# Moving the first tile's q and k into the last slots of a first attention, and the expert selection within them

## What is computed

```python
x = x + tanh(g_xattn[0]) * attention0(layernorm(x), ctx)    # 32 query, 8 key/value heads of 128, rope, softmax
x = x + tanh(g_ffn[0])  * ffn0(layernorm(x))                # 4-bit weights, 8-bit activations, silu(gate) * up, down
x = x + tanh(g_xattn[1]) * attention1(layernorm(x), ctx)    # over the 512 channels of each sequence
x = x + tanh(g_ffn[1])  * moe(layernorm(x))                 # base product + 4 of 16 low-rank experts with a router

def attention1(x, init):                     # per sequence, init is the context, 64 x 512
    q = Wq @ init + bq;  k = Wk @ init + bk  # 64 x 512 each
    A = softmax(q.T @ k)                     # 512 x 512
    v = Wv @ x + bv
    return A applied to v

def moe(x):
    y = x @ W_base.T + b_base
    contribs = (x @ A_e.T) @ B_e.T * 2       # rank 8, for the four active experts e
    alpha = softmax(log(prior[active] + 1e-12) + router(x)[active])
    return y + sum_e alpha_e * contribs_e
```

## Time and profile before

| | us |
|---|---|
| median of 3 timed runs | 848.2 (847.93 to 850.28) |
| the profiled execution | 856.15 |
| its span, first to last instruction | 854.3 |
| TensorE busy in the span | 816.7 (96%) |
| VectorE | 559.4 (65%) |
| ScalarE | 464.3 (54%) |
| GpSimd | 503.1 (59%) |
| mean granted TensorE clock | 0.983 of full |

### The profile page before, as it was taken

The page is one execution under the profiler, slowest core; times in us unless marked ns, Lnnn a source line. Parts: engine busy times, 40 slices in busy tenths (PEclk is TensorE's granted clock), DMA queues, the critical chain, the costliest instruction groups (busy, mean ns, idle before and its releaser), DMA issues. The chain is left out here.

```text
span 854.3 us, 13778 instructions
## 1 busy us (share of the span) xinstructions
PE 816.7 (96%) x5009; PEld 657.5 (77%) x5025; DVE 559.4 (65%) x1041; ACT 464.3 (54%) x874; POOL 503.1 (59%) x432
## 2 busy tenths in 40 slices
PE   6799999999999999999999999998968999999996
PEld 5688888888888888888888888886835677777785
DVE  3767656656566465564565545454779999999852
ACT  2465445554455454444544444332368899888761
POOL 1557744666555676456665557533057787877762
PEclk9999999999999999999999999998889999999998
DMA  8520331422413133131231104128044313321300
GB/s 260 136 87 26 111 87 38 125 54 76 124 35 100 44 89 102 38 94 43 65 109 43 38 5 26 50 37 305 2 111 119 83 48 90 85 76 25 87 26 25
DMA packets 74307, 66.77 MB, mean 78 GB/s; under 512 B 35920, under 2 KB 53552, under 8 KB 73856
## 3 DMA queue, kind: packets, MB, share of 16 engines
q1 hardware_dynamic: 73280, 65.55, 28.3%
q10 hardware_dynamic: 960, 0.33, 0.1%
HBM read 49.04 MB, written 6.34 MB: 65 GB/s over the span
## 5 line engine op out<-in xcount | busy, mean ns | idle before, releaser
L917 DVE SCALAR_TENSOR_TENSOR x_res<-bank,gate,x_res 128x512 f32<-128x512 f32 x128 | 95.7, 747 | 96.9 <-PE bank L505 96.5
L1155 POOL TENSOR_TENSOR prob<-prob,row_inv 128x512 f32<-128x512 f32 x32 | 33.5, 1046 | 197.5 <-DVE row_inv L913 197.5
L1141 POOL TENSOR_TENSOR rope_swap<-rope_swap,trig 128x512 f32<-128x512 f32 x80 | 103.6, 1295 | 35.5 <-ACT rope_swap L688 35.5
L78 PE MATMUL bank<-xnT_hi,wq_hi 128*128 128x512 f32 (+1 forms) x264 | 106.0, 402 | 1.0 <-DVE xnT_lo L852 1.0
L500 PE MATMUL bank<-wo_hi,oT_hi 128*128 128x512 f32 x256 | 102.9, 402 | 3.7 <-DVE x_res L917 3.5
L80 PE MATMUL bank<-xnT_hi,wq_lo 128*128 128x512 f32 (+1 forms) x264 | 103.7, 393 | 0.0
L79 PE MATMUL bank<-xnT_lo,wq_hi 128*128 128x512 f32 (+1 forms) x264 | 103.1, 391 | 0.0
L501 PE MATMUL bank<-wo_lo,oT_hi 128*128 128x512 f32 x256 | 102.4, 400 | 0.0
L888 DVE TENSOR_TENSOR rope_cos<-bank,trig 128x512 f32<-128x512 f32 x80 | 54.6, 683 | 71.5 <-PE bank L80 71.5
L687 ACT COPY rope_swap<-bank 64x512 f32<-64x512 f32 x80 | 46.8, 585 | 88.5 <-DVE rope_cos L888 87.9
L1147 POOL TENSOR_TENSOR q_rope<-rope_cos,rope_swap 128x512 f32<-128x512 f32 x64 | 83.4, 1303 | 5.0
(11 more groups left out here) (225 smaller groups left out, 1954.5 us busy)
## 6 DMA issues: line engine op xcount, KB each, us to landing
wq_raw<-in_L_xattn_wq SPq DMA_DIRECT2D x16, 512.0 KB, 4.2
wo_raw<-in_L_xattn_wo SPq DMA_DIRECT2D x16, 512.0 KB, 3.9
xn<-in_L_ffn_Wd SPq DMA_DIRECT2D x16, 256.0 KB, 3.4
b_ctx<-in_ctx SPq DMA_DIRECT2D x32, 128.0 KB, 2.7
b_k_twice<-b_qk_hi SPq DMA_DIRECT2D x32, 128.0 KB, 2.4
w_T_dram<-w_out SPq DMA_DIRECT2D x28, 128.0 KB, 2.3
w_T<-w_T_dram SPq DMA_DIRECT2D x2, 1376.0 KB, 8.1
xn<-in_L_ffn_Wg SPq DMA_DIRECT2D x10, 256.0 KB, 4.0
```

The lines of the kernel that those rows point to most:

```text
L78: pe.matmul(out, a_hi, b_hi, start=first, stop=False)
L917: dve.scalar_tensor_tensor(out=K.x[:, t, :], in0=wo_ps[t % 2][:, :], scalar=K.gate[:, 0:1], in1=K.x[:, t, :], op0=ALU.mult, op1=ALU.add).t ...
L1141: pool.tensor_tensor(out=sw, in0=sw, in1=sin_b, op=ALU.mult).then_inc(s_rope, 1)
```

## The change

Seven edits, and the lists of the tail written anew.

1. VectorE's expert selection, both halves, stands after the four accumulates of slot 30 and not among them.
2. ScalarE's split of tile 0's context (first_split_hi, twice) moves from the tail to the end of its slot 30, the low part from the tail's head on GpSimd to its queue behind the last normalise; GpSimd's reciprocal root for the first four x tiles now stands behind it, and the four clears of k_lo behind that.
3. q and k of tile 0 (first_qk) are made between the first and second tile sum of unit 31 in the attention's own banks; first_hi_qk and first_lo_qk follow on ScalarE and VectorE.
4. SyncE issues tile 0's ten copies in the first block.
5. low_T is cut in two: channels 0 and 1 after the second tile sum, 2 and 3 and the spread products after the third. first_x_transpose and low_b_select come between that and the fourth sum, no longer at the end.
6. ln_prior is ScalarE's last step of the first block; the second then starts with a table load for tanh.
7. qk_lo and ctx_raw/x3 change places in SBUF.

```diff
@@ sync, after load_context of tile 0
+            sp.wait_ge(M.s_k_zero, 4)
+            for par in range(2):
+                sp.wait_ge(M.s_qk_lo[par], 1)
+                duplicate_tile(sp, M, 0, par)
@@ tensor
-                    if tl == 1 and between is not None:
-                        between()
+                    if between is not None:
+                        between(tl)
...
+            def first_qk(par):
+                if par == 0:
+                    pe.wait_ge(s_w_qkv, 4)
+                    pe.wait_ge(s_w_qkv_lo, 1)
+                    pe.wait_ge(s_oT_lo, 2 * 2 * NPAIR)
+                pe.wait_ge(M.s_ctx_lo[par], 1)
+                pe.matmul(av[par][:, :], M.qk_w_hi[:, :], M.ctx_split[par][:, :], start=True, stop=False)
+                pe.matmul(av[par][:, :], M.qk_w_lo[:, :], M.ctx_split[par][:, :], start=False, stop=True).then_inc(M.s_qk[par], 1)
...
-            output(2 * NPAIR - 1, low_T)
-            low_b_select()
-            first_x_transpose()
+            def between(tl):
+                if tl == 0:
+                    first_qk(0)
+                    first_qk(1)
+                if tl == 1:
+                    low_T((0, 1))
+                if tl == 2:
+                    low_T((2, 3))
+                    first_x_transpose()
+                    low_b_select()
+
+            output(2 * NPAIR - 1, between)
@@ scalar
+            def first_split_hi(par):
+                act.wait_ge(M.s_ctx[par], 32)
+                act.copy(M.ctx_split[par][:, :], M.ctx_raw[par][:, :]).then_inc(M.s_ctx_hi[par], 1)
+            def first_hi_qk(par):
+                act.wait_ge(M.s_qk[par], 1)
+                act.activation(M.qk_hi[par][:, :], av[par][:, :], ACT.Identity, bias=K.W1.bias[:, :]).then_inc(M.s_qk_hi[par], 1)
...
                         base_high_part(0)
+                        first_split_hi(0)
+                        first_split_hi(1)
...
             bT_copy()
+            first_hi_qk(0)
+            first_hi_qk(1)
             shift_tile(act, M, 0)
             int_tile(act, M, 0)
             low_part()
+            first_xT_copy()
             low_b_hi()
-            first_xT_copy()
+            ln_prior()
@@ vector
-                    if U == 2 * NPAIR - 2 and k == 0:
-                        selection_of_experts()
-                    if U == 2 * NPAIR - 2 and k == 1:
-                        selection_matrices()
...
+                if U == 2 * NPAIR - 2:
+                    selection_of_experts()
+                    selection_matrices()
...
             front_tile(dve, K, M, 0)
+            base_low_part(3)
+            first_lo_qk(0)
             accumulate(last + 1, UT + 1)
-            base_low_part(3)
+            first_lo_qk(1)
@@ gpsimd
             run_groups(body)
+            pool.wait_ge(s_prob, 2 * NPAIR)
+            for par in range(2):
+                pool.wait_ge(M.s_ctx_hi[par], 1)
+                pool.tensor_tensor(out=M.ctx_split[par][S:P, :], in0=M.ctx_raw[par][S:P, :], in1=f32(M.ctx_split[par][S:P, :]),
+                                   op=ALU.subtract).then_inc(M.s_ctx_lo[par], 1)
+            pool.wait_ge(M.s_ctx_lo[1], 1)
             pool.wait_ge(s_x_stat, 2 * UT + 1)
...
+            pool.wait_ge(s_av, 2 * NPAIR)
+            for i in range(2):
+                for par in range(2):
+                    pool.memset(f32(M.k_lo[i][par][:, :]), 0.0).then_inc(M.s_k_zero, 1)
@@ tail, the five lists written anew, the first calls of TensorE's
             up_mm(0, 0)
-            qk(0, 0)
+            logits(0, 0)
```

## The result

The changed kernel takes 842.65 us (median of 6 runs, 841.42 to 845.44). The kernel before, timed beside it, took 850.60 us (6 runs, 847.93 to 851.82). The ratio is 0.9918, with a 95% interval of 0.9892 to 0.9943: a gain of some 7 us (4.8 to 9.2), where 11 were forecast. The profiled execution took 845.44 us, its span is 843.6 us, 10.7 us shorter than that of before. A second set of 6 runs on another chip gave 0.9916 (0.9886 to 0.9947).

A forecast was written before the change was run, and what follows sets the result against it. Bounds: an idle gap and half-rate clock in the last slots, a tail head short of work, then VectorE up to 683 us and TensorE after. Sum -7.0 - 4.5 + 0.5 = -11.0; off the 848.2 median, 837.2 us; range 830.5 to 845.

The forecast's parts named there:

- the middle gives the head start back: Rival, tail: the new order may lose 4 us over eight tiles, giving 842 us; chance 0.17.
- Selection after the updates, -3.5: Slot 30: TensorE's idle 3.54 us goes, and the moved selection is covered by the score products; -3.5 us.
- The half rate behind it, -4.3: 590.00 to 600.25 us, clock 0.51 after the idle gap: full clock returns; -4.3 us, ends -5.1 and -1.0.
- the half rate is not in the timed runs: Rival: half-rate stretches belong to the profiled execution, so -4.3 and -2.5 cannot be won; 844 us, chance 0.10.
- ScalarE waits for the context, +1.8: First attention's last slots: ScalarE's context copies delay its copy of the last transposed probabilities; +1.8 us, ends 0 and +3.
- I don't count on an earlier landing: Context loads: issued earlier, but behind the feed-forward weight loads, so landing was still taken at 599.2 us.
- Four products for q and k, +0.9: Ahead of the second of the last tile sums: four products of 0.23 us each, inputs ready; +0.9 us.
- Low-rank products in two pieces, -2.5: 614.15 to 620.90 us: splitting keeps the clock up or lets it fall late; -2.5 us, from -3.4 to 0.
- the end of the block, +0.6: First block's end: VectorE's update and low part of B follow the last sum, 2.0 us for 1.4; +0.6 us.
- Start of the tail, 7.0 us earlier: First block's terms together: 3.5 + 4.3 - 1.8 - 0.9 + 2.5 - 0.6 = 7.0 us, tail starting near 616.4.
- Head of the tail, -4.5: Tail's head: VectorE loses two operations (1.4 us) and 3.1 us idle; -4.5 us, ends 0 and -10.
- its new order, +0.5: Tail's rewritten order: last tile's down projection, update and statistics come three score steps later; +0.5 us, from 0 to +1.5.

The follow-up runs named there:

- the filled gap: Kernel before, selection left among the updates, plus 14 unread TensorE products between the second and third tile sum of output(29): 848.59 us against 850.36, ratio 0.9962.
- the kernel with late loads: Changed kernel with the loads of the down weights and row scales issued behind the four context loads: 841.36 us, ratio 0.9892 to the kernel before.
- TensorE's added work: Changed kernel with the up products of the tail's second and third tile run twice on TensorE: 846.25 us, ratio 0.9953 to the kernel before.
- the old order: Changed kernel with the tail's instruction orders of the kernel before, less the moved calls: 844.02 us; with context loads also issued first: 841.83 us.
- the kernel with late loads and one piece: Changed kernel with down-weight and row-scale loads behind the context loads and low-rank products in one piece as before: 843.12 us, ratio 0.9916.

## Why the prediction was right, and where its sizes were off

The direction and the place were right: faster by more than 0.3%, and 842.65 lies in the range. The likeliest case, 834 to 840 us with a chance of 0.45, did not come. The nearest named case is "the middle gives the head start back" (842, 0.17), and its mechanism isn't what the traces show, so that its number fits is luck. The forecast of 837.2 is 5.4 us off, for two reasons. The median of before that it was taken off, 848.2, came from three runs; over 6 to 23 runs on each chip it is 849.7 to 850.6, and the 850.6 beside the changed kernel makes 2.4 us of it. The other 3 us are in the sum: -11.0, and about -7 to -8 measured.

*Selection after the updates, -3.5:* right. The gap of 3.54 us is gone, and the selection is covered by the score products but for 0.1 to 0.2 us (586.26 against 586.14).

*The half rate behind it, -4.3:* the mechanism is shown (the filled gap), the size was taken from one execution. In the timed runs it is 1.9 to 4.7 us, most likely about 3, and that for both half-rate stretches together, for which the forecast had 4.3 + 2.5 = 6.8. The rival "the half rate is not in the timed runs" was half right: it is in them, as their granted clocks show (0.986 and 0.987, against 0.990 and 0.992 without the gap), and shorter.

*ScalarE waits for the context, +1.8:* right in place and engine; 2.49 us of waiting, and 2.8 us from mark to mark by the kernel with late loads. The step put the landing at 8.6 us after issue, as in the earlier trace rows. It took 11.1, because the loads were issued earlier, behind the same backlog. "I don't count on an earlier landing" was right.

*Four products for q and k, +0.9:* right; in the changed kernel's trace they start at 603.04 and the next product at 603.97, without a wait.

*Low-rank products in two pieces, -2.5, and the end of the block, +0.6:* the failed step. It priced the half rate from 614.15 to 620.90 and credited it to the split. But that stretch is gone with the selection's edit alone (clock 1.00 over 600.35 to 604.81), where the products still run in one piece. What the split itself does is +0.35 us by trace, and nothing in the runs. The two terms of the clock were counted as if each had its own cause; in the runs each of two edits that act on the gap alone (the selection moved, the gap filled) removed both, by one trace each. With the gap back and the split in place the second stretch is absent as well, so the split may have an effect on it that has nothing left to remove here. Why the second stretch goes with the first, over 10 us later, stays open.

*Start of the tail, 7.0 us earlier:* 6.3 by the first pair of traces, which is luck: that trace of the kernel before is the one with the long half rate. Against its second trace (39.45 us from mark to mark) the two of the changed kernel (36.55 and 35.35) gain 2.9 and 4.1. Of the 6.8 us of the two clock terms that second trace has 3.3, and the context cost up to 1 us more than its term.

*Head of the tail, -4.5, and its new order, +0.5:* sign and size were about right, 3.2 us by ten traces for 4.0; the first pair alone says 1.6. The head start was 8 us at the first row maximum, and the step took 4.5 for what a chain over VectorE could keep. That chain is not the whole story: TensorE's added work comes through too, though it has 4.26 us of idle time in the middle of the tail (40.74 busy of 45.00). The chain of waits of the changed kernel shows it as well: near 650 us, where the prediction wanted VectorE, both engines are in it (start, duration, what):

```profile
641.00 0.77 PE gate_ps L1537 x4
...
645.52 0.86 PE up_ps L1545 x4
...
649.16 3.64 PE av_ps L1606 x64
654.91 0.69 DVE b_neg_max L2096
```

So the middle gives back some 5 of the 8 us, and the rival by which it gives back all that the tail gains does not hold. Nor is an early row maximum worth much by itself: with the old order it stands 10.9 and 9.6 us behind the first gate product, with the new one 3.9 (618.52 - 614.62), and the tail is no longer with the old (226.8 and 227.5). Where between 20 and 200 us of the tail each microsecond goes was not pinned down.

*The rule on table loads:* the Trainium skill (ScalarE: Activation LUTs, "What ACT_TABLE_LOAD costs") has a drain of 1.38 us beside the load of 1.28. In the kernel with late loads and one piece the load starts at 609.37, lasts 1.28 and the logarithm begins at 610.67, 0.02 us behind it, and the copy ahead of the load ends at 609.35, 0.02 us before it: no drain on either side. In the earlier trace rows, too, the logarithm follows its load by 0.02 us.

In all: the selection's place carries the gain of 7 us. The move of q, k and the logarithm, the split and the new order together are worth 1.0 to 4.4 us while the gap is there, and add nothing that can be measured once the selection is moved. By the traces the tail saves some 3 us then, and the end of the first block loses as much against the selection alone (36.55 and 35.35 for 32.46), more than half of it in the wait for the context. With that wait removed the kernel is at 841.4 and 841.8 us (ratios 0.9892 and 0.9876), the best of this study.

## What to carry to other kernels

A short job in an in-order queue costs more than its length when it waits for an input there: look for what stands ahead of the engine that sets the end, and move the job to where its engine waits anyway. A term sized from one execution's clock needs a second trace of the same kernel before it is counted, and two stretches at half rate are not two independent gains. The mean granted clock of each timed execution tells whether the profiled one is typical (0.983 here, where the median was 0.986 to 0.988). When work is moved earlier, its loads have to be moved ahead of the backlog too; otherwise the wait moves to whatever is queued behind the first copy.

## What the runs showed that was not expected

The stretch at half rate behind one and the same idle gap (3.54 and 3.55 us in the kernel before, 3.54 with the selection back) lasted about 10, 3.5 and 13.7 us. Its length is no property of the kernel: the first two are the same code.

Filling an idle gap of TensorE with 14 products that nobody reads made the kernel 1.9 to 4.7 us faster. With the gap's time lost all the same, that is the half rate's price alone.

Four loads of 128 KB took 11.1 us (median) from issue to landing behind the loads of the down weights and row scales, and 3.1 us ahead of them. ScalarE's wait of 6.48 us and TensorE's of 2.49 us hung on that order of issue.
